# Two edits in a four-layer decoder on one core: the attention of layer 2 with split key sums, logarithm roots and shared copies, and a state-space loop whose softplus is put ahead of a masked copy

## The chip, the core and the metric

The kernel runs on one core of a Trainium2 chip. Five engines work side by side, each in the order of its own program: TensorE (PE, with its weight loads shown as PEld), VectorE (DVE), ScalarE (ACT), GpSimd (POOL) and SyncE (SP, which only starts transfers here). They wait for each other by semaphores. The metric is the device time of one launch in microseconds, the median of several runs. Lower is better.

## What is computed

The program is a decoder of four layers on x of shape 8 x 256 x 128, each with attention, cross attention and a feed-forward part. Two of its twelve stages are touched.

The state space (part of layer 1's attention) runs 4 Mamba layers over 8 sequences, 32 units in all. A unit has a step size by softplus, a causal convolution, a masked overlap of the B and C projections, decays, and a result that passes a gate and a norm.

The wide cross attention (layer 2) has 8 sequences of 256 queries and 256 keys, 16 heads of 64, with a mean-square norm of every head of queries and keys:

```python
def rms_norm(x, w):
    var = jnp.mean(jnp.square(x), axis=-1, keepdims=True)
    return x * jax.lax.rsqrt(var + EPS) * w
qh = rms_norm((q @ Wq).reshape(b, l, HEADS, HEAD_DIM).transpose(0, 2, 1, 3), q_norm_w)
kh = rms_norm((kv @ Wk).reshape(b, s, HEADS, HEAD_DIM).transpose(0, 2, 1, 3), k_norm_w)
vh = (kv @ Wv).reshape(b, s, HEADS, HEAD_DIM).transpose(0, 2, 1, 3)
scores = jnp.where(mask, jnp.einsum('bhld,bhsd->bhls', qh, kh) * (1.0 / np.sqrt(HEAD_DIM)), NEG_INF)
o = jnp.einsum('bhls,bhsd->bhld', jax.nn.softmax(scores, axis=-1), vh)
```

## The kernel before

Every stage hands each engine a list of instructions in a fixed order; nothing is scheduled at run time.

**The wide attention** (class `Wide`) has 64 steps: 8 sequences by 8 pairs of heads, w = 0 to 7. In step p, PE forms the scores of pair p in banks 0 and 1 (`score_pe`); DVE takes the row maxima and makes the exponential's biases (`maximum_dve`, L3045 and L3049); ACT takes the exponentials (`weigh_act`, L3150). PE's scores of step p+1 wait for these exponentials, since they use the same two banks. DVE then sums the exponentials of step p-1 (`inverse_dve`, L3065 to L3070), POOL scales them (`scale_pool`, L3241), PE turns those of step p-2 (`turn_pe`, L2928), DVE copies one bank of them and ACT the other (`copy_dve` L3056, `copy_act` L3159), and PE multiplies those of step p-3 by the values (`values_pe`).

Between these stand the pieces that prepare the next sequence, by a table: `SCHEDULE` says in which of the 8 steps each is done. P00 to P11 are the key projections (token half, column half), copied by ACT; Q0 to Q3 the queries; KS the sums of the squared keys over each head, whose squares POOL makes (`squares_pool`, L3236); KR a square root on ACT (L3174) and KD a reciprocal (L3085) and the scaling of the two key halves on DVE (L3089); T00 to T11 the turned keys, copied by DVE (L3111); M and X the queries' mean squares; QR and QD their root (L3177) and reciprocal (L3092); V0 to V3 the values, copied and masked by DVE (L3104); B0 and B1 the output product of the sequence before. The first two PE pieces of a step are "early": on each engine they stand after the exponentials (ACT) or the sums (DVE), and ahead of the copies of the turned weights. The others stand at the step's end. PE's pieces go through three banks in turn. The `Sqrt` of a root needs another table of ACT than the `Exp` of the steps, so a table load (ACT_TABLE_LOAD) stands ahead of each root and ahead of the next exponential.

**The state space** (class `StateSpace`) runs one iteration n per unit. In an iteration DVE does, in this order: the masked copy of the overlap (`overlap_dve`, L1902 and L1903, which waits for PE); the decays' product (`weights_dve`, L1908, the other half of which POOL does under the same line); the first tap of the convolution (L1890); the final product into XNT (`final_dve`, L1942); more taps (L1893); the sums (L1932, L1936); and the inputs (L1923). In every second iteration the softplus of the next two units is worked in between: five small operations (`start_dve`, L1594 to L1602) after the masked copy, four steps of a series (L1608) after the decays' product, and the rest after the first tap. The softplus starts from an exponential that ACT makes at the iteration's start (L1587).

Of the kernel before, what the change touches and what calls it, by code (L numbers as in the profile page):

```python
# [1631 lines left out]
class StateSpace:  # L1632
# [311 lines left out]
    def dve(self, dve):  # L1944
# [877 lines left out]
class Wide:  # L2822
# [12 lines left out]
    SCHEDULE = (("P00", "P01", "Q0"), ("P10", "P11", "Q1"), ("Q2", "Q3", "KS"), ("M", "V0", "KR", "KD"), ("B0", "V1"),  # L2835
                ("T00", "T01", "X"), ("T10", "T11", "V2", "QR", "QD"), ("B1", "V3"))
# [3 lines left out]
    def __init__(self, k):  # L2840
# [21 lines left out]
        on_pe = [piece for piece in self.place if piece[0] not in ("KS", "KR", "KD", "QR", "QD")]  # L2862
# [25 lines left out]
    def read(self, piece):  # L2888
# [3 lines left out]
        return signal.at(*piece)  # L2892
# [3 lines left out]
    def score_pe(self, pe, p):  # L2896
        s, (b, w) = self.k.s, divmod(p, NWIDE)
        q, key = self.side(self.Q, b), self.side(self.K, b)
        if w == 0:
            pe.wait_ge(*self.read(("Q3", b)))  # L2900
            pe.wait_ge(*self.read(("T11", b)))
# [32 lines left out]
    def values_pe(self, pe, p):  # L2934
        s, (b, w) = self.k.s, divmod(p, NWIDE)
        if w == 0:
            pe.wait_ge(*self.read(("V3", b)))
# [103 lines left out]
    def maximum_dve(self, dve, p, o):  # L3041
# [5 lines left out]
        if w == 0 and o == 0:  # L3047
            dve.wait_ge(*s.rstd.at("queries", b))
# [23 lines left out]
    def piece_dve(self, dve, piece):  # L3072
# [3 lines left out]
        if name == "KS":  # L3076
            for t in range(HALVES):
                dve.wait_ge(*s.pool.at("squares", b, t))
                dve.tensor_reduce(self.kms[:, t * H:(t + 1) * H], self.ksquares[t].rearrange("p (h d) -> p h d", d=HW), AXX,
                                  ALU.add).then_inc(*s.stats.up("keys", b, t))  # L3080
            dve.wait_ge(*s.stats.at("keys", b, HALVES - 1))
            dve.tensor_scalar(self.kms, self.kms, 1.0 / HW, 1e-5, ALU.mult, ALU.add).then_inc(*s.variance.up("keys", b))
        elif name == "KD":
            dve.wait_ge(*s.deviation.at("keys", b))
            dve.reciprocal(self.kms, self.kms).then_inc(*s.rstd.up("keys", b))  # L3085
            dve.wait_ge(*s.rstd.at("keys", b))
            for t in range(HALVES):
                x = self.raw[t].rearrange("p (h d) -> p h d", d=HW)
# [132 lines left out]
    def pool(self, pool):  # L3221
# [1108 lines left out]
```

## Time and profile before

| | |
|---|---|
| Time of the kernel before, median of 3 runs | 2303.56 us (2299.27 to 2307.39) |
| Profiled execution: its own time | 2310.8 us |
| Profiled execution: span from first to last instruction | 2309.0 us |
| Busy: PE, DVE, ACT, POOL | 1907.6, 1584.6, 1307.4, 646.3 us |
| Mean granted TensorE clock | 0.904 |
| State-space loop in the trace | about 521 to 960 us |
| Wide attention in the trace | about 1378 to 1797 us |

The span is the profiler's stretch from the first to the last instruction; 1.8 us of that execution lie around it. Busy time is a sum over stages with different limits, so each stage has to be read by itself.

### The profile page before, as it was taken

What the parts mean: (1) busy time and instruction counts of PE and PEld (TensorE: products, weight loads), DVE (VectorE), ACT (ScalarE), POOL (GpSimd) and SP (SyncE); (2) the same over time, 40 slices, a digit from 0 to 9 for tenths busy, and PEclk for the clock granted to TensorE, in tenths of its full rate; (3) what the DMA queues carried; (4) which work ended last, traced back from release to release, by engine and by line L of the source; (5) the groups of instructions that cost most, each with busy time, mean ns of one, the idle gap of its engine ahead of it and who ended that gap; (6) DMA issues with size and microseconds to landing.
All of it is one profiled execution on the core that took longest, in us unless ns stands there. A gap on an engine that the chain in (4) does not pass through costs nothing.

```text
span 2309.0 us, 37826 instructions
## 1 busy us (share of the span) xinstructions
PE 1907.6 (83%) x13360; PEld 1271.5 (55%) x13360; DVE 1584.6 (69%) x3689; ACT 1307.4 (57%) x2688; POOL 646.3 (28%) x616
## 2 busy tenths in 40 slices
PE   7999766979999999849864388899888997679886
PEld 5777652446777777524452254556555676434465
DVE  5777685866767767458659948888888457568543
ACT  5777433766777777517755236676665312337622
POOL 3332003104433333342004532334334001131043
PEclk9999887999999999969986689999999898779897
DMA  4000005400000000034101000000000100254112
GB/s 191 1 2 2 1 0 152 141 34 5 1 1 1 1 1 1 1 91 147 56 8 68 0 1 1 1 1 1 1 1 1 52 4 1 95 159 132 43 35 78
DMA packets 80155, 87.39 MB, mean 38 GB/s; under 512 B 6578, under 2 KB 70115, under 8 KB 79073
## 3 DMA queue, kind: packets, MB, share of 16 engines
q1 hardware_dynamic: 78625, 82.49, 11.3%
q0 software_dynamic: 1344, 2.49, 0.4%
q8 instruction: 109, 1.79, 0.3%
q14 instruction: 77, 0.63, 0.1%
HBM read 54.39 MB, written 30.70 MB: 37 GB/s over the span
## 4 chain that ended last, share of the span: by engine, by line
PE 50%; DVE 31%; issue 8%; POOL 5%; ACT 5%; DMA 2%; SPq 0%; DVEq 0%; POOLq 0%; ACTq 0%
PE bank L469 42%; DVE scratch L1221 5%; PE bank L653 2%; DVE scratch L3045 2%; DVE scratch L3065 2%; PE bank L368 2%; POOL w_early L3241 1%; DVE stats L245 1%; PE bank L693 1%; POOL w_early L3236 1%; DVE w_keep L1893 1%; DVE w_early L2497 1%; PE bank L1190 1%; DVE XN L3089 1%; DMA scratch<-parts 1%
## 5 line engine op out<-in xcount | busy, mean ns | idle before, releaser
L469 PE MATMUL bank<-scratch 64*128 64x256 bf16 (+7 forms) x3056 | 340.9, 307 | 83.2 <-DMA scratch<-parts 39.8
L1221 DVE TENSOR_REDUCE scratch<-bank 128x2 f32<-128x512 f32 x384 | 244.6, 686 | 83.5 <-PE bank L469 80.6
L469 PEld LDWEIGHTS bank<-scratch 64*128 64x128 bf16 (+4 forms) x3056 | 183.9, 122 | 212.1 <-DVE scratch L1221 73.6
L469 PE MATMUL bank<-w_keep,scratch 128*128 128x128 f32 (+4 forms) x1760 | 246.6, 331 | 26.8 <-DVE scratch L1936 12.1
L469 PE MATMUL bank<-XNT,w_keep 128*128 128x256 f32 (+4 forms) x800 | 238.6, 438 | 6.8 <-POOL w_keep L2131 4.6
L1307 ACT ACTIVATE w_keep<-bank 128x512 f32<-128x512 f32 x384 | 212.5, 597 | 53.6 <-PE bank L469 45.7
L469 PEld LDWEIGHTS bank<-w_keep,scratch 128*128 128x128 f32 (+3 forms) x1760 | 183.7, 185 | 92.9 <-issue 63.5
L469 PE MATMUL bank<-w_early,scratch 64*128 64x256 f32 (+3 forms) x1152 | 168.9, 355 | 42.4 <-ACT w_early L3150 26.0
L469 PEld LDWEIGHTS bank<-XNT,w_keep 128*128 128x128 f32 x800 | 150.2, 197 | 59.9 <-issue 30.4
L469 PEld LDWEIGHTS bank<-w_early,scratch 64*128 64x128 f32 (+3 forms) x1152 | 122.6, 189 | 89.2 <-issue 32.3
L469 PE MATMUL bank<-w_keep 128*32 128x256 f32 (+1 forms) x1600 | 125.2, 388 | 8.8 <-ACT w_keep L1307 5.4
L469 PE MATMUL bank<-scratch,w_early 128*128 128x256 f32 (+2 forms) x416 | 124.0, 442 | 10.2 <-DVE scratch L2492 3.8
L795 ACT ACTIVATE scratch<-bank,scratch 128x256 f32<-128x256 f32 x256 | 100.3, 475 | 54.9 <-DVE scratch L721 54.9
L3150 ACT ACTIVATE w_early<-bank,scratch 128x256 f32<-128x256 f32 x172 | 83.0, 563 | 84.3 <-DVE scratch L3049 84.2
L3241 POOL TENSOR_TENSOR w_early<-w_early,scratch 128x1024 f32<-128x1024 f32 x43 | 81.4, 1893 | 173.5 <-DVE scratch L3070 173.5
L721 DVE TENSOR_REDUCE scratch<-bank 128x2 f32<-128x512 f32 x128 | 82.5, 686 | 61.7 <-PE bank L469 61.6
L469 PE MATMUL bank<-XNT,w_early 128*128 128x256 f32 (+1 forms) x384 | 119.1, 441 | 4.5 <-ACT XNT L383 1.6
L368 PE MATMUL bank<-w_keep,XN 128*128 128x128 f32 x192 | 49.3, 435 | 78.9 <-DVE XN L318 76.1
L3045 DVE TENSOR_REDUCE scratch<-bank 128x2 f32<-128x512 f32 x128 | 87.6, 685 | 25.4 <-PE bank L469 25.2
L469 PEld LDWEIGHTS bank<-scratch,w_early 128*128 128x128 f32 x416 | 72.2, 199 | 51.2 <-issue 30.8
L469 PEld LDWEIGHTS bank<-XNT,w_early 128*128 128x128 f32 x384 | 73.2, 201 | 46.0 <-issue 32.1
L735 POOL TENSOR_TENSOR scratch<-scratch 128x1024 f32<-128x1024 f32 x32 | 61.5, 1951 | 127.2 <-DVE scratch L751 127.2
(452 smaller groups left out, 3974.5 us busy)
## 6 DMA issues: line engine op xcount, KB each, us to landing
scratch<-parts SPq DMA_DIRECT2D x24, 1024.0 KB, 5.0
parts<-scratch SPq DMA_DIRECT2D x192, 96.0 KB, 2.5
parts<-scratch SPq DMA_DIRECT2D x96, 64.0 KB, 2.1
w_early<-pack_l3f SPq DMA_DIRECT2D x1, 5206.0 KB, 16.3
w_keep<-pack_l2f SPq DMA_DIRECT2D x1, 2124.0 KB, 12.5
w_early<-pack_mamba SPq DMA_DIRECT2D x1, 2120.0 KB, 19.2
w_keep<-pack_l2x SPq DMA_DIRECT2D x1, 2049.0 KB, 7.8
w_keep<-taps SPq DMA_DIRECT2D x4, 512.0 KB, 5.6
```

Of the source, the lines that this page charges most:

```text
L368: t = pe.transpose(k.bank[q][:, j * P:(j + 1) * P], src(i), k.w["ident"])
L469: return pe.matmul(out, lhsT, rhs, start=start, stop=stop, skip_group_check=True)
L653: m = pe.transpose(self.k.bank[3 + o][:, c * S + t * P:c * S + (t + 1) * P], self.expo[g % 4][:, t * S + c * P:t * S + (c + 1) * P], self. ...
L721: dve.tensor_reduce(self.neg[g % 4], self.scores(g)[:, :].rearrange("p (t s) -> p t s", s=S), AXX, ALU.max, negate=True).then_inc(*s.maxed ...
L735: return pool.tensor_tensor(self.kron[n][t].rearrange("p (h i j) -> p h i j", i=HD, j=HD), a, c, ALU.mult)
L795: a = act.activation(self.expo[g % 4][:, t * S:(t + 1) * S], self.scores(g)[:, t * S:(t + 1) * S], ACT.Exp, bias=self.neg[g % 4][:, t:t + 1])
L1221: dve.tensor_reduce(neg[:, :, h], self.k.bank[5 - g % 2][:, :].rearrange("p (t s) -> p t s", s=S), AXX, ALU.max, negate=True).then_inc(*s. ...
L1307: act.activation(self.expo[g % 8], k.bank[g % 4][:, :], ACT.Exp, scale=HD ** -0.5).then_inc(*s.weighed.up("e", g))
L3045: dve.tensor_reduce(neg, self.k.bank[o][:, :].rearrange("p (t s) -> p t s", s=S), AXX, ALU.max, negate=True).then_inc(*s.maxed.up("x", p, o))
L3065: dve.tensor_reduce(sums, self.by_row(p), AXX, ALU.add).then_inc(*s.stats.up("sums", p))
L3150: a = act.activation(self.weights(p, o)[:, t * S:(t + 1) * S], self.k.bank[o][:, t * S:(t + 1) * S], ACT.Exp, bias=self.bias[p % 2][:, o * ...
L3241: pool.tensor_tensor(ex, ex, self.sums[p % 2].unsqueeze(2).to_broadcast([P, 2 * HALVES, S]), ALU.mult).then_inc(*s.pool.up("scaled", p))
```

## The change

Wide attention. KS becomes KS0 and KS1, one token half each, in steps 1 and 2, and POOL squares a half ahead of the scaling of its step instead of behind it. KR moves from step 3 to step 2, and takes `Ln` (with the mean's factor and the small constant inside) and `Exp` with factor -0.5 instead of `Sqrt`; so the reciprocal and the variance operation of DVE go, and no table load is left in the loop. KD becomes KD0 and KD1, in steps 3 and 4. QR does the same with `Ln` and `Exp`, and QD goes. V1, V3, T01 and T11 are copied by ACT instead of DVE. State space: the softplus' start and first four series steps stand ahead of the masked copy.

```diff
+            if soft:
+                soft.start_dve(dve, n)
+                soft.series_dve(dve, n, 0, 4)
             if there(prep):
                 self.overlap_dve(dve, prep)
-            if soft:
-                soft.start_dve(dve, n)
-            if there(prep):
                 self.weights_dve(dve, prep)
-            if soft:
-                soft.series_dve(dve, n, 0, 4)
...
-    SCHEDULE = (("P00", "P01", "Q0"), ("P10", "P11", "Q1"), ("Q2", "Q3", "KS"), ("M", "V0", "KR", "KD"), ("B0", "V1"),
-                ("T00", "T01", "X"), ("T10", "T11", "V2", "QR", "QD"), ("B1", "V3"))
+    SCHEDULE = (("P00", "P01", "Q0"), ("P10", "P11", "Q1", "KS0"), ("Q2", "Q3", "KS1", "KR"), ("M", "V0", "KD0"), ("B0", "V1", "KD1"),
+                ("T00", "T01", "X"), ("T10", "T11", "V2", "QR"), ("B1", "V3"))
+    ON_ACT = ("V1", "V3", "T01", "T11")
...
+        if name[0:2] == "KS":
+            t = digits[0]
+            dve.wait_ge(*s.pool.at("squares", b, t))
+            dve.tensor_reduce(self.kms[:, t * H:(t + 1) * H], self.ksquares[t].rearrange("p (h d) -> p h d", d=HW), AXX,
+                              ALU.add).then_inc(*s.stats.up("keys", b, t))
+        elif name[0:2] == "KD":
+            t = digits[0]
+            x = self.raw[t].rearrange("p (h d) -> p h d", d=HW)
             dve.wait_ge(*s.deviation.at("keys", b))
...
         if name == "KR":
-            act.wait_ge(*s.variance.at("keys", b))
-            act.activation(self.kms, self.kms, ACT.Sqrt).then_inc(*s.deviation.up("keys", b))
+            act.wait_ge(*s.stats.at("keys", b, 1))
+            act.activation(self.kms, self.kms, ACT.Ln, bias=k.small[:, 0:1], scale=1.0 / HW).then_inc(*s.scalar.up("keys", b))
+            act.wait_ge(*s.scalar.at("keys", b))
+            act.activation(self.kms, self.kms, ACT.Exp, scale=-0.5).then_inc(*s.deviation.up("keys", b))
...
+        elif name[0] == "V" and name in self.ON_ACT:
+            t, part = divmod(digits[0], 2)
+            act.wait_ge(*s.projected.at(*piece))
...
+            act.activation(self.values(b)[:, t, 8 * part:8 * part + 8, :], bank[:, :].rearrange("p (h d) -> p h d", d=HW), ACT.Copy,
+                           scale=self.keep[:, b * HALVES + t:b * HALVES + t + 1]).then_inc(*s.stacked.up(*piece))
...
         for p in range(self.STEPS):
             b, w = divmod(p, NWIDE)
-            self.scale_pool(pool, p)
             if w in (0, 1) and b + 1 < B:
                 self.squares_pool(pool, b + 1, w)
+            self.scale_pool(pool, p)
...
-        pre_norm_act(k, e, ACT.Exp)
+        pre_norm_act(k, e)
+        e.preload_act_table_set("natural_log_exp_and_others")
```

On DVE, in the state space's iteration with a softplus, the order changes as follows (L1902 and L1903 are the masked copy, L1594 to L1602 the softplus' start, L1608 its series, L1908 the decays' product):

```order
-L1902 TENSOR_TENSOR scratch<-bank,w_keep 128x256
-L1903 COPY scratch<-bank 128x128
 L1594 TENSOR_SCALAR scratch<-scratch 128x16
 L1596 RECIPROCAL scratch<-scratch 128x16
 L1598 TENSOR_TENSOR scratch<-scratch 128x16
 L1600 TENSOR_TENSOR scratch<-scratch 128x16
 L1602 TENSOR_SCALAR scratch<-scratch 128x16
-L1908 TENSOR_TENSOR scratch<-scratch 128x512
 L1608 SCALAR_TENSOR_TENSOR scratch<-scratch 128x16 x4
+L1902 TENSOR_TENSOR scratch<-bank,w_keep 128x256
+L1903 COPY scratch<-bank 128x128
+L1908 TENSOR_TENSOR scratch<-scratch 128x512
```

Nine small operations now stand ahead of the copy, and the copy and the product stand together.

On DVE in the wide attention, step 3 of a sequence before, from the sums of the exponentials (L3065) to the next step's maxima (L3045): L3104 is V0, L3056 the copy of the turned weights, L3085 and L3089 are KD.

```order
L3065 TENSOR_REDUCE scratch<-w_early 128x4
L3067 SCALAR_TENSOR_TENSOR scratch<-w_early,scratch 128x4
L3070 RECIPROCAL scratch<-scratch 128x4
L3104 TENSOR_SCALAR scratch<-bank,scratch 128x512
L3056 COPY scratch<-bank 128x512
L3085 RECIPROCAL scratch<-scratch 128x32
L3089 TENSOR_TENSOR XN<-XN,scratch 128x1024 x2
L3045 TENSOR_REDUCE scratch<-bank 128x2
```

The same stretch in the changed kernel, where L3100 is V0, L3057 the copy and L3086 KD0:

```order
L3066 TENSOR_REDUCE scratch<-w_early 128x4
L3068 SCALAR_TENSOR_TENSOR scratch<-w_early,scratch 128x4
L3071 RECIPROCAL scratch<-scratch 128x4
L3100 TENSOR_SCALAR scratch<-bank,scratch 128x512
L3057 COPY scratch<-bank 128x512
L3086 TENSOR_TENSOR XN<-XN,scratch 128x1024
L3046 TENSOR_REDUCE scratch<-bank 128x2
```

The reciprocal is gone, and the scaling of the second key half has moved into step 4, behind that step's copy; in both steps the sums, after which POOL starts its scaling, stand a copy and a value or output piece ahead of it.

On ACT in the wide attention, from the last copies of step 3 to the next exponentials before (L3174 is the keys' root, L3150 an exponential):

```order
L3159 ACTIVATE scratch<-bank 128x512
L3166 ACTIVATE CX<-bank 128x256
L3174 ACT_TABLE_LOAD
L3174 ACTIVATE scratch<-scratch 128x32
L3150 ACT_TABLE_LOAD
L3150 ACTIVATE w_early<-bank,scratch 128x256 x4
```

In the changed kernel the root stands at the end of step 2, as L3170 and L3172:

```order
L3155 ACTIVATE scratch<-bank 128x512
L3170 ACTIVATE scratch<-scratch,small 128x32
L3172 ACTIVATE scratch<-scratch 128x32
L3146 ACTIVATE w_early<-bank,scratch 128x256 x4
L3212 ACTIVATE w_early<-bank 128x512
```

Both table loads are gone from this place, and the root stands ahead of step 3's exponentials instead of behind them.

## Rows read from the trace of the kernel before

**Rows 1.** Busy time in the wide attention, with granted clock (windows, all engines)

```profile
core 0: us, PE busy (x) PEld busy (x) DVE busy (x) ACT busy (x) POOL busy (x), PEclk, DMA share, GB/s
...
1380.00:1785.00 405.00, 354.39 (x2264) 230.04 (x2264) 338.22 (x682) 268.39 (x529) 148.93 (x79) 0.96 0.00 1
```

**Rows 2.** Wide attention, PE in order of time: start, duration, idle before

```profile
1558.11 1.13 PE L469 MATMUL bank<-w_early,scratch 64*128 64x256 f32 x8
...
1562.99 1.70 PE L469 MATMUL bank<-w_early,scratch 64*128 64x256 f32 x16
...
1571.01 2.08 PE L469 MATMUL bank<-w_early,scratch 64*128 64x256 f32 x8 [2.94 <-ACT w_early L3150]
...
1579.63 1.14 PE L469 MATMUL bank<-w_early,scratch 64*128 64x256 f32 x8
...
1584.39 1.14 PE L469 MATMUL bank<-w_early,scratch 64*128 64x256 f32 x8
...
1589.82 1.14 PE L469 MATMUL bank<-w_early,scratch 64*128 64x256 f32 x8
...
1596.49 1.13 PE L469 MATMUL bank<-w_early,scratch 64*128 64x256 f32 x8 [0.81 <-ACT w_early L3150]
...
1602.42 1.13 PE L469 MATMUL bank<-w_early,scratch 64*128 64x256 f32 x8
```

**Rows 3.** Wide attention, DVE in order of time, steps 2 and 3

```profile
1559.28 0.69 DVE L3045 TENSOR_REDUCE scratch<-bank 128x2 f32<-128x512 f32 x1 [2.04 <-PE bank L469]
...
1566.76 1.22 DVE L3079 TENSOR_REDUCE scratch<-w_early 128x16 f32<-128x1024 f32 x1 [1.79 <-POOL w_early L3236]
...
1568.11 0.68 DVE L3045 TENSOR_REDUCE scratch<-bank 128x2 f32<-128x512 f32 x1
...
1571.32 0.74 DVE L3104 TENSOR_SCALAR scratch<-bank,scratch 128x512 f32<-128x512 f32 x1
...
1573.78 0.35 DVE L3085 RECIPROCAL scratch<-scratch 128x32 f32<-128x32 f32 x1 [1.12 <-ACT scratch L3174]
1574.17 2.36 DVE L3089 TENSOR_TENSOR XN<-XN,scratch 128x1024 f32<-128x1024 f32 x2
```

**Rows 4.** Wide attention, POOL in order of time: three of its 64 scalings

```profile
1407.19 1.89 POOL L3241 TENSOR_TENSOR w_early<-w_early,scratch 128x1024 f32<-128x1024 f32 x1 [19.49 <-DVE scratch L3070]
...
1571.48 1.89 POOL L3241 TENSOR_TENSOR scratch<-scratch 128x1024 f32<-128x1024 f32 x1 [4.76 <-DVE scratch L3070]
...
1756.24 1.89 POOL L3241 TENSOR_TENSOR scratch<-scratch 128x1024 f32<-128x1024 f32 x1 [2.51 <-DVE scratch L3070]
```

**Rows 5.** The bias operation, L3049: duration ns min/median/max

```profile
L3049 DVE TENSOR_TENSOR scratch<-scratch x128: 161/164/1216, 1400.5 to 1781.1; 128x2 f32<-128x2 f32 x128
```

**Rows 6.** State space, DVE in order of time: an iteration with softplus, one without

```profile
705.55 0.43 DVE L1902 TENSOR_TENSOR scratch<-bank,w_keep 128x256 f32<-128x256 f32 x1 [3.67 <-PE bank L469]
...
706.09 0.17 DVE L1594 TENSOR_SCALAR scratch<-scratch 128x16 f32<-128x16 f32 x1
...
706.57 0.98 DVE L1598 TENSOR_TENSOR scratch<-scratch 128x16 f32<-128x16 f32 x1
...
708.36 0.69 DVE L1908 TENSOR_TENSOR scratch<-scratch 128x512 f32<-128x512 f32 x1
708.96 0.80 DVE L1608 SCALAR_TENSOR_TENSOR scratch<-scratch 128x16 f32<-128x16 f32 x4
709.68 0.61 DVE L1890 TENSOR_SCALAR w_keep<-w_keep,w_early 128x256 f32<-128x256 f32 x2
...
711.42 0.42 DVE L1942 TENSOR_TENSOR XNT<-bank,scratch 128x256 f32<-128x256 f32 x1
...
720.83 2.09 DVE L1890 TENSOR_SCALAR w_keep<-w_keep,w_early 128x256 f32<-128x256 f32 x2
```

**Rows 7.** State space, POOL in order of time, the iteration with softplus

```profile
706.25 1.27 POOL L1908 TENSOR_TENSOR scratch<-scratch 128x512 f32<-128x512 f32 x1 [3.27 <-DVE scratch L1903]
```

**Rows 8.** State space, ACT in order of time: the softplus' exponential

```profile
703.54 0.21 ACT L1587 ACTIVATE scratch<-scratch 128x16 f32<-128x16 f32 x1
```

**Rows 9.** Who waited for whom, 540 to 940 us: total, times, longest

```profile
PE bank L469 <- DVE XNT L1942: 16.0, 14, 1.2
```

More of the change, by code:

```diff
@@ L2822 @@
 class Wide:
-    SCHEDULE = (("P00", "P01", "Q0"), ("P10", "P11", "Q1"), ("Q2", "Q3", "KS"), ("M", "V0", "KR", "KD"), ("B0", "V1"),
-                ("T00", "T01", "X"), ("T10", "T11", "V2", "QR", "QD"), ("B1", "V3"))
+    SCHEDULE = (("P00", "P01", "Q0"), ("P10", "P11", "Q1", "KS0"), ("Q2", "Q3", "KS1", "KR"), ("M", "V0", "KD0"), ("B0", "V1", "KD1"),
+                ("T00", "T01", "X"), ("T10", "T11", "V2", "QR"), ("B1", "V3"))
+    ON_ACT = ("V1", "V3", "T01", "T11")
+    UNBANKED = ("KS0", "KS1", "KR", "KD0", "KD1", "QR")
     LAG = 2
@@ L2861, in __init__ @@
                         self.place[name, b] = d * NWIDE + step if d >= 0 else -1
-        on_pe = [piece for piece in self.place if piece[0] not in ("KS", "KR", "KD", "QR", "QD")]
+        on_pe = [piece for piece in self.place if piece[0] not in self.UNBANKED]
         self.number = {piece: n for n, piece in enumerate(on_pe)}
@@ L2891, in read @@
         signal = {"P": s.stacked, "Q": s.stacked, "M": s.stacked, "V": s.formed, "T": s.formed, "X": s.formed, "B": s.added}[name[0]]
-        return signal.at(*piece)
+        return (s.stacked if name in self.ON_ACT else signal).at(*piece)
     def score_pe(self, pe, p):
@@ L2899, in score_pe @@
         if w == 0:
-            pe.wait_ge(*self.read(("Q3", b)))
+            pe.wait_ge(*self.read(("T10", b)))
             pe.wait_ge(*self.read(("T11", b)))
@@ L2936, in values_pe @@
         if w == 0:
+            pe.wait_ge(*self.read(("V2", b)))
             pe.wait_ge(*self.read(("V3", b)))
@@ L3047, in maximum_dve @@
         if w == 0 and o == 0:
-            dve.wait_ge(*s.rstd.at("queries", b))
+            dve.wait_ge(*s.deviation.at("queries", b))
         dve.tensor_tensor(bias, neg, self.root(b)[:, w // 4, :, w % 4, o], ALU.mult).then_inc(*s.biased.up("x", p, o))
@@ L3075, in piece_dve @@
         digits = [int(x) for x in name[1:] if x.isdigit()]
[L3076 to L3083, printed above, removed]
-            dve.wait_ge(*s.deviation.at("keys", b))
[L3085 to L3088, printed above, removed]
-                dve.tensor_tensor(x, x, self.kms[:, t * H:(t + 1) * H].unsqueeze(2).to_broadcast([P, H, HW]), ALU.mult).then_inc(*s.normed.up("keys", b, t))
-        elif name == "QD":
-            dve.wait_ge(*s.deviation.at("queries", b))
-            dve.reciprocal(self.qms[b % 2], self.qms[b % 2]).then_inc(*s.rstd.up("queries", b))
+        if name[0:2] == "KS":
[6 more added lines that the diff above has]
+            x = self.raw[t].rearrange("p (h d) -> p h d", d=HW)
+            dve.wait_ge(*s.deviation.at("keys", b))
+            dve.tensor_tensor(x, x, self.kms[:, t * H:(t + 1) * H].unsqueeze(2).to_broadcast([P, H, HW]), ALU.mult).then_inc(*s.normed.up("keys", b, t))
+        elif name in self.ON_ACT:
+            pass
         elif name[0] == "X":
@@ L3168, in piece_act @@
     def piece_act(self, act, piece):
-        s, (name, b) = self.k.s, piece
+        k, s, (name, b) = self.k, self.k.s, piece
         bank = self.bank(piece) if piece in self.number else None
@@ L3201, in act @@
         s = self.k.s
-        act.wait_ge(*s.vector.at("gain"))
+        act.wait_ge(*s.vector.at("keep"))
         for piece in self.pieces(-1):
```

13 lines of the change are left out of this document (12 added, 1 removed).

## The prediction

> **What bounds the kernel now.** The two stages have different limits, so I read each by itself, in this order: busy times by stretch, each engine in order of time, then who waits for whom.
>
> In the wide attention PE is busy 354 and DVE 338 of 405 us, at a mean granted clock of 0.96 [rows 1]. Neither is full, so the order of time has to tell. POOL's scaling of the first pair of heads stands at 1407.19 us for sequence 0 and at 1756.24 us for sequence 7 [rows 4]: seven sequences take 349.05 us, 49.9 each. In a middle one, PE's score groups mark the steps [rows 2]. PE itself works 5.93 us in step 0 (1596.49 to 1602.42), 4.88 in step 2, 5.08 in step 3 (1562.99 until it stops at 1571.01 less the 2.94 idle), 4.76 in step 5, 5.43 in step 6 and 5.86 in step 7 (without its 0.81 idle). Step 1 has the same pieces as step 0, and step 4 nearly those of step 7, 5.9. The sum is 43.8 us: what PE alone would take. The missing six us lie around step 3. DVE waits 1.79 us for POOL's squares in step 2 [rows 3], 1.12 us for ACT's root in step 3 [rows 3], and has much to do there; from one maximum at 1559.28 to the next at 1568.11 are 8.8 us. PE, whose scores need the exponentials behind those maxima, stands idle 2.94 us, and its next score group reads 2.08 us instead of 1.13 [rows 2]: the clock has fallen to its lower level for a moment. So this stage is DVE's, by steps 2 and 3, and PE would be next.
>
> In the state space PE waits for DVE's final product (L1942) in 14 iterations, 16.0 us in all [rows 9], about 1.15 each. That product stands at 711.42 us, late because the softplus is worked in ahead of it, while DVE sat idle 3.67 us just before, for PE's overlap [rows 6].
>
> **The change: state space.** The softplus' input is ready at 703.75 us (703.54 plus 0.21) [rows 8], DVE is idle until 705.55 [rows 6]. The nine operations now cost: the start from 706.09 to 708.36, 2.27 us, and four series steps from 708.96 to 709.68, 0.72 us [rows 6], 2.99 in all. But of the start, 0.8 us is L1598 alone, 0.98 us for 16 numbers a row where its neighbour L1594 takes 0.17 [rows 6]; it ends as POOL's 1.27 us product of 706.25 does [rows 7]. The next operation meets the POOL instruction behind. Ahead of the copy POOL has nothing of the kind to do, so I take 1.8 us: 703.8 to 705.6, which just fills the hole; the masked copy is late by 0.1 at most.
>
> From the copy to the final product are 5.87 us now (705.55 to 711.42). 2.99 leave. Something comes in: the first tap (L1890, two operations) takes 0.61 us here, but 2.09 in the iterations without softplus, where it meets POOL's product [rows 6]. With the softplus gone from in front of it, it meets it here too: plus 1.5. So 5.87 - 2.99 + 1.5 = 4.4, and with the 0.1 of lateness the product comes at 710.0 to 710.1 instead of 711.42: 1.3 earlier, which covers PE's wait of 1.15. Fourteen times that is the 16.0 us of [rows 9]. Bounds: nothing, if the softplus' start meets POOL again or ACT's exponential is late; 18 if PE's next waits shrink too. I take 16, the wait as measured.
>
> **The change: wide attention.** Costs by slot, from start to start. A bare DVE step is 3.8 us: maxima and sums 3.21 (1568.11 to 1571.32), and the copy, which with V0 ends at 1573.78 less 1.12, 1.34 for the two [rows 3]: 0.65 for a value piece, 0.6 for a copy. A key sum is 1.1 to 1.2 (L3079, 1.22), a key scaling 1.15 (half of L3089's 2.36) [rows 3]. Turned-key copies I take at 0.6 like the other copy, an output piece at 0.55.
>
> What leaves DVE per sequence: two value pieces 1.3, two key copies 1.2, reciprocals and variance 0.8, and the waits 1.79 and 1.12. What stays by step: 3.8, 4.9, 5.0, 5.6, 5.5, 4.5, 6.1, 4.3; sum 39.7 against PE's 43.8. ACT gains about four copies and two small operations, some 3 us, and loses the four table loads; where it waits for DVE's biases nearly every step it stays covered. Only step 2 brings it close (exponentials, Q2, Q3, copies and the root: 5.4 us). PE's program keeps its order and length.
>
> Would PE then run without a stop? The loop through the exponentials is short enough: maximum 1.17 after its score (1558.11 to 1559.28), next score 2.90 after the maximum (1568.11 to 1571.01) [rows 2, 3], 4.1 together, under PE's shortest step. By the steps alone, yes. But two small key operations move. KD0 and KD1 now stand 4.4 to 4.5 us behind the step's first maximum, and POOL's scaling begins 3.37 behind it (1568.11 to 1571.48) and takes 1.89 [rows 3, 4], so it is under way. Before, the scaling of 1571.48 was over when L3089 began at 1574.17. A DVE operation with two operands in SBUF that meets POOL seems to wait for it: L1598 above, and the bias operation, whose median is 164 ns and whose longest is 1216 [rows 5].
>
> The Trainium skill says so, and it speaks against this placing: "SBUF — State Buffer", section "Who interferes with whom", has a VectorE instruction with two SBUF inputs shut out while a GpSimd instruction reads SBUF, for all of that instruction. The traced L1598 agrees (0.98 us). By that rule a sequence takes the 45.6 us worked out next; if KD escaped it, 43.8.
>
> So KD0 ends at 5.22 + 1.15 = 6.4 behind its step's maximum instead of 5.6, and KD1 likewise, 6.4 instead of 5.5. The squares, which POOL now makes directly behind a scaling in steps 0 and 1, hold the next step's first bias operation by 0.3 and 0.6 us. Followed step by step (score at t, maximum at D, D the later of t + 1.17 and the end of DVE's step, next t the later of PE's end and D + 2.90), with t = 0 in step 0: scores at 5.9, 11.9, 16.8, 21.9, 28.2, 34.4, 39.8, and 45.6 for the next sequence; maxima at 1.2, 7.1, 13.0, 18.6, 25.0, 31.4, 36.0, 42.1. PE stops only ahead of step 6, for 1.4 us. The same rule with the steps of before gives 50.1, where 50.2 is seen, so I add 0.2 a sequence for what it lacks. Sequence 0 has no output pieces: 44.6. Six times 45.6, plus 44.6, plus 1.4: 319.6 against 349.05, a gain of 29.5. Sequence 7 has no pieces at all but outputs; it stays as it is. The first sequence's preparation loses a table load and a reciprocal on its chain and shares copies, all of which I put at 2 us (0 to 3, the load being 1.3 and the rest already beside PE).
>
> Sum: 16 + 29.5 + 2 = 47.5 us. Against the profiled execution, 2310.8 us with 1.8 around its span, that gives 2263.3; the median of the runs is 7.2 lower than that execution, so 2303.56 - 47.5 = 2256.
>
> **Rivals.** (a) As forecast, 2249 to 2263: 0.55. (b) KD is not held by POOL, or the holds fall into slack: PE runs through, 43.8 a sequence and 42.8 for sequence 0, a gain of 43.5, so 2242; against it L1598 and the longest L3049. 0.13. (c) PE's pause ahead of step 6 grows past what the clock forgives. A pause of 2.94 us brought the lower level, and score groups of 2.08 us; 0.81 did not [rows 2]. The low level cost the score group 0.95 us, and I count as much for the piece behind it: 1.9 us in each of six sequences, or as much in new small waits on the key sums or roots, makes 2268; my 1.4 lies between. 0.15. (d) The softplus ahead of the copy pays nothing, because the copy, and with it POOL's product and the tap, come later by as much: 2272. 0.10. (e) Both gains melt to under 7 us together: 0.04. (f) The other side, by one mechanism, the clock. If the new rhythm gave PE four pauses of over 2 us a sequence instead of one, each with the 1.9 of (c) behind it, seven sequences would lose 4 x 3.9 x 7 = 109 us, and with the gains of 47.5 the time is 2365. It decides from 54.5 lost, 7.8 us a sequence. The steps above have one pause, not four: 0.03. That the change does not do what it says is excluded for the loads: its order on ACT has none in the loop.
>
> 0.3% of the time, 7 us, is about what a measurement here can tell from nothing. Faster is (a) to (d), 0.93; within it (e), 0.04; slower (f), 0.03. The range must leave out at most 2 in 10: from (b)'s 2242, a us below for the 18 of the state space, to (d)'s 2272, plus one: 2241 to 2273.
>
> **What would show it.** L1598 near 0.17 us in nearly all iterations, L1890 near 2.1 in all, PE's wait for L1942 gone. In the wide attention no table load, no wait for the squares, key scalings of 1.9 to 2.1 us instead of 1.2, scaling of pair 0 every 45.6 us, PE idle mostly ahead of step 6, granted clock near 1.0. I am wrong if PE's step work is longer than read (its ends are modelled), if ACT becomes late in step 2 or 3, or if the copies that ACT takes over hold a bank that PE wants.

## The result, and the profile after

The changed kernel takes 2250.05 us (median of 4 runs, 2242.86 to 2250.55) against 2303.76 us for the one before beside it (2299.27 to 2307.39): a ratio of 0.9761, 95% interval 0.9734 to 0.9787. That is 53.7 us less; 47.5 were forecast. The profiled execution took 2249.74 us (span 2247.9, mean granted clock 0.913).

The busy times by stretch of the changed kernel: the stretch that holds the state space, the wide attention up to POOL's first scaling, its seven sequences, and its end.

```profile
core 0: us, PE busy (x) PEld busy (x) DVE busy (x) ACT busy (x) POOL busy (x), PEclk, DMA share, GB/s
337.03:981.93 644.90, 572.41 (x4000) 400.03 (x4000) 456.15 (x1174) 449.88 (x958) 219.16 (x215) 0.94 0.11 30
1347.47:1382.60 35.13, 28.99 (x120) 16.84 (x122) 20.70 (x46) 22.17 (x45) 5.68 (x3) 0.84 0.00 0
1382.60:1697.40 314.80, 295.18 (x1992) 190.68 (x1990) 288.17 (x553) 215.64 (x478) 130.05 (x69) 1.00 0.00 1
1697.40:1738.49 41.09, 32.91 (x248) 23.30 (x244) 29.51 (x62) 20.44 (x44) 15.14 (x8) 0.96 0.01 1
```

Cut at the same operations (a layer norm's variance, the first scalings of sequences 0 and 7), the two profiled executions compare so, in us:

| stretch | before | after | less |
|---|---|---|---|
| the one with the state space | 667.39 | 644.90 | 22.5 |
| in it, a pair of iterations, one with softplus and one without | 26.97 | 25.70 | 1.27 |
| wide attention to its first scaling | 36.0 | 35.2 | 0.8 |
| seven sequences | 349.05 | 314.8 | 34.3 |
| in them, a middle sequence | 50.2 | 45.35 | 4.9 |
| end of the wide attention | 41.1 | 41.1 | 0 |
| everything else | 1215.5 | 1212.0 | 3.5 |

In the wide attention PE now is busy 295 of 315 us at a granted clock of 1.00, where [rows 1] had 354 of 405 at 0.96. PE in order of time, in a middle sequence, shows all of its pauses:

```profile
1563.95 1.14 PE L469 MATMUL bank<-w_early,scratch 64*128 64x256 f32 x8
...
1568.83 1.70 PE L469 MATMUL bank<-w_early,scratch 64*128 64x256 f32 x16
...
1573.86 1.14 PE L469 MATMUL bank<-w_early,scratch 64*128 64x256 f32 x8
...
1579.87 1.14 PE L469 MATMUL bank<-w_early,scratch 64*128 64x256 f32 x8
...
1582.29 1.09 PE L2928 MATMUL bank<-w_keep,scratch 128*128 128x128 f32 x8 [0.26 <-POOL scratch L3255]
...
1586.13 1.13 PE L469 MATMUL bank<-w_early,scratch 64*128 64x256 f32 x8 [1.15 <-ACT w_early L3146]
...
1588.56 1.09 PE L2928 MATMUL bank<-w_keep,w_early 128*128 128x128 f32 x8 [0.27 <-POOL w_early L3255]
```

The 2.94 us that PE stood idle in step 3 and the score group of 2.08 us behind them [rows 2] are gone. So is what followed that group, sixteen matmuls that were also at the lower level; before and after they read:

```profile
1573.02 3.78 PE L469 MATMUL bank<-w_keep,CX 128*128 128x128 f32 x16
...
1574.92 2.05 PE L469 MATMUL bank<-w_keep,scratch 128*128 128x128 f32 x16
```

From score group to score group, step 3 falls from 8.02 to 5.03 us, which is the pause, and step 4 from 8.62 to 6.01, which is nearly all clock. More than half of the 4.9 us that a sequence gains is thus the clock behind the pause and not the pause; steps 5 to 7 together give 0.7 back. Step 2 keeps its 4.88. One pause of some size is left, 1.15 us ahead of step 6, where the forecast had 1.4. With 0.26 and 0.27 for two scalings that is 1.68, and 45.35 less 1.68 is 43.7 us of PE's own work, forecast as 43.8.

On DVE, in order of time, one finds what holds those exponentials back (L3071 is the reciprocal that POOL's scaling waits for, L3050 the bias operation, L3086 a key scaling):

```profile
1556.39 0.18 DVE L3071 RECIPROCAL scratch<-scratch 128x4 f32<-128x4 f32 x1
...
1559.92 0.49 DVE L3050 TENSOR_TENSOR scratch<-scratch 128x2 f32<-128x2 f32 x1
...
1565.84 0.82 DVE L3050 TENSOR_TENSOR scratch<-scratch 128x2 f32<-128x2 f32 x1
...
1575.17 1.88 DVE L3086 TENSOR_TENSOR XN<-XN,scratch 128x1024 f32<-128x1024 f32 x1
...
1581.27 2.04 DVE L3086 TENSOR_TENSOR XN<-XN,scratch 128x1024 f32<-128x1024 f32 x1
```

and on POOL, beside the last two:

```profile
1574.08 1.89 POOL L3255 TENSOR_TENSOR w_early<-w_early,scratch 128x1024 f32<-128x1024 f32 x1 [3.03 <-DVE scratch L3071]
...
1580.34 1.89 POOL L3255 TENSOR_TENSOR scratch<-scratch 128x1024 f32<-128x1024 f32 x1 [4.37 <-DVE scratch L3071]
```

Key scalings last 1.88 and 2.04 us, where half of L3089's 2.36 was 1.18 [rows 3]. POOL's scaling runs from 1574.08 to 1575.97, and the key scaling issued at 1575.17 ends at 1577.05, 1.08 behind it: it reads like one that could not begin until POOL was through. All fourteen key scalings of the seven sequences end 1.08 or 1.09 us behind the end of a POOL scaling, whether they were issued 0.43 or 1.09 us behind its start. The bias operation shows the squares that POOL now makes earlier, as 0.49 and 0.82 instead of 0.16, so held by 0.33 and 0.66 (forecast 0.3 and 0.6).

In the state space, DVE in order of time, an iteration with softplus:

```profile
697.24 0.18 DVE L1594 TENSOR_SCALAR scratch<-scratch 128x16 f32<-128x16 f32 x1 [1.90 <-ACT scratch L1587]
...
697.74 0.17 DVE L1598 TENSOR_TENSOR scratch<-scratch 128x16 f32<-128x16 f32 x1
...
699.10 0.42 DVE L1902 TENSOR_TENSOR scratch<-bank,w_keep 128x256 f32<-128x256 f32 x1
...
700.37 2.10 DVE L1890 TENSOR_SCALAR w_keep<-w_keep,w_early 128x256 f32<-128x256 f32 x2
...
703.61 0.42 DVE L1942 TENSOR_TENSOR XNT<-bank,scratch 128x256 f32<-128x256 f32 x1
```

L1598 takes 0.17 us instead of 0.98, and the two taps 2.10 instead of 0.61, as [rows 6] had them in the other iterations. From the copy to the final product are 4.51 us (forecast 4.4, before 5.87). Who waits for whom, 540 to 930 us, in total, times and longest:

```profile
PE bank L469 <- DVE scratch L1936: 10.5, 15, 1.7
PE bank L469 <- DVE XNT L1942: 1.3, 1, 1.3
```

Of PE's 14 waits for the final product [rows 9] one is left, the first, ahead of the steady rhythm; 13 are gone. The wait for L1936 is the one that stays, 0.63 us in a pair where it was 0.71; in total it was 12.1 us before.

### The profile page after: what moved, and what is told of

It is laid out like the page before. It is cut to its first block, busy times and chain, and to the rows that moved or that the text cites. A ratio compares the mean times of both kernels' runs of the same rounds, so it can differ in the third digit from the quotient of the medians.

```text
span 2247.9 us, 37788 instructions
## 1 busy us (share of the span) xinstructions
PE 1885.0 (84%) x13360; PEld 1256.4 (56%) x13360; DVE 1581.0 (70%) x3633; ACT 1284.4 (57%) x2705; POOL 654.6 (29%) x616
## 4 chain that ended last, share of the span: by engine, by line
PE 53%; DVE 29%; ACT 6%; issue 6%; POOL 2%; DMA 2%; SPq 0%; DVEq 0%; POOLq 0%; ACTq 0%
PE bank L469 45%; DVE scratch L1221 5%; PE bank L653 2%; ACT XN L1994 2%; PE bank L2928 2%; PE bank L368 2%; DVE scratch L3046 1%; DVE w_keep L1890 1%; DVE scratch L3066 1%; DVE stats L245 1%; PE bank L693 1%; DVE XN L3086 1%; DVE w_keep L1893 1%; DVE w_early L2495 1%; PE bank L1190 1%
## 5 line engine op out<-in xcount | busy, mean ns | idle before, releaser
L469 PE MATMUL bank<-w_keep,scratch 128*128 128x128 f32 (+4 forms) x1760 | 245.4, 330 | 24.9 <-DVE scratch L1936 10.5
L469 PE MATMUL bank<-XNT,w_keep 128*128 128x256 f32 (+4 forms) x800 | 238.1, 437 | 6.9 <-POOL w_keep L2129 4.7
L1893 DVE SCALAR_TENSOR_TENSOR w_keep<-w_keep,w_early 128x256 f32<-128x256 f32 x192 | 96.6, 552 | 0.1
```

What stands on the lines that cost most here:

```text
L469: return pe.matmul(out, lhsT, rhs, start=start, stop=stop, skip_group_check=True)
L1893: o = dve.scalar_tensor_tensor(out=yv[:, j, :], in0=xv[:, j, tap:tap + S], scalar=scale, in1=yv[:, j, :], op0=ALU.mult, op1=ALU.add)
```

## The experiments

All ratios are to the kernel before, run beside each. "Pair" is the pair of iterations of the table above, "sequence" a middle one of the seven, "wide attention" the whole stage in the trace, its preparation and end included.

| kernel | median us (range) | ratio [95%] | pair | sequence | wide attention |
|---|---|---|---|---|---|
| softplus_only | 2287.33 (2279.7–2290.04) | 0.9921 [0.9897, 0.9945] | 25.70 | 50.23 | 426.1 |
| wide_only | 2263.75 (2261.26–2271.09) | 0.9842 [0.9806, 0.9879] | 26.97 | 45.35 | 391.0 |
| keys_first | 2247.54 (2235.24–2249.26) | 0.976 [0.9729, 0.9791] | 25.70 | 44.08 | 383.7 |
| tap_first | 2251.13 (2247.98–2254.09) | 0.9775 [0.9741, 0.9808] | 25.74 | 45.35 | 391.0 |
| copies_on_dve | 2257.99 (2251.7–2262.61) | 0.9806 [0.977, 0.9842] | 25.70 | 46.84 | 400.6 |
| squares_behind | 2287.78 (2281.91–2294.12) | 0.9928 [0.9904, 0.9952] | 25.70 | 50.4 | 426.3 |
| square_roots | 2265.19 (2264.5–2268.43) | 0.9835 [0.98, 0.9871] | 25.70 | 47.7 | 404.8 |
| keys_again | 2248.55 (2241.27–2250.21) | 0.9749 [0.9723, 0.9774] | 25.70 | 44.08 | 385.2 |
| after_again | 2243.05 (2239.85–2252.6) | 0.974 [0.9712, 0.9768] | 25.70 | 45.35 | 389.8 |
| both_first | 2248.35 (2236.62–2251.87) | 0.9749 [0.9721, 0.9776] | 25.74 | 44.08 | 385.3 |

The kernel before took 2305.23 us beside rows one to four, 2304.9 beside rows five to seven and 2305.29 beside rows eight to ten; its wide attention took 426.1 us.

**One part of the change at a time.** softplus_only is the kernel before with the state space's edit alone; wide_only is the changed kernel with that edit undone, so:

```diff
+            if there(prep):
+                self.overlap_dve(dve, prep)
             if soft:
                 soft.start_dve(dve, n)
-                soft.series_dve(dve, n, 0, 4)
             if there(prep):
-                self.overlap_dve(dve, prep)
                 self.weights_dve(dve, prep)
+            if soft:
+                soft.series_dve(dve, n, 0, 4)
```

> The kernel before with the state space's edit alone. My theory: the two edits sit in different stages and add up, and this one takes PE's wait for the final product, 1.15 us in each of 14 iterations, and a little of the next wait: a pair of units in 25.7 us instead of 26.97, some 19 to 22 us in all, so about 2283; L1598 at 0.17 us and L1890 at 2.1 us in every iteration; the wide attention as before. Rival: the gain in the state space comes in part from the other edit or from run-to-run differences; then it is 8 us or less.

> The changed kernel with the softplus put back behind the masked copy. My theory: the wide attention's gain stands alone, 31 to 35 us, a sequence in 45.3 us instead of 50, so about 2270; the state space as before, 26.97 us a pair. Rival: the two edits share a resource or a clock state, and this run differs from the changed kernel by clearly more or less than what the other run gains (sum of the two gains off by over 7 us from 54).

Measured: 17.9 us for the first (2305.23 to 2287.33) and 41.5 for the second. Each part's rhythm is the same alone as with the other: 25.70 us a pair with either wide attention, 45.35 a sequence with either state space. The sum, 59.4, and the 53.7 of both together differ by no more than the intervals (5.5 to 8.4 us to either side) allow. The second is larger than the 31 to 35 us that I had expected, but in the trace the stage itself is 35.1 us shorter (391.0 for 426.1); the rest lies in code that was not touched.

The medians are too coarse for the size of the state space's part, so I take it from the trace. From the first unit's final product to the last one's are 384.91 us in wide_only and 368.33 in the changed kernel, 16.6 less: thirteen pairs at 1.27, and no change in the last iterations. In softplus_only, keys_first, keys_again and after_again it is 368.3 to 369.1. Ahead of the first product nothing is clearly won (237.4 us of the stretch in wide_only, 235.8 to 238.1 in these five). The stretch as a whole is a poorer witness; in wide_only, where nothing in it was changed, it took 660.76 us instead of 667.39. The kernel before had two pieces of that stretch at the lower clock:

```profile
core 0: us, PE busy (x) PEld busy (x) DVE busy (x) ACT busy (x) POOL busy (x), PEclk, DMA share, GB/s
...
959.17:969.41 10.24, 9.16 (x13) 3.94 (x14) 1.12 (x2) 3.66 (x6) 0.53 (x1) 0.50 0.00 0
552.98:556.39 3.41, 3.41 (x12) 1.97 (x9) 1.34 (x2) 3.02 (x5) 3.33 (x4) 0.50 0.02 5
```

**Key scalings away from POOL.** KD0 and KD1 stand directly behind the step's two maxima, ahead of the sums of the exponentials that POOL's scaling waits for.

```diff
                 self.maximum_dve(dve, p, 1)
+            early, late = self.split(p)
+            keys, late = [x for x in late if x[0][0:2] == "KD"], [x for x in late if x[0][0:2] != "KD"]
+            for piece in keys:
+                self.piece_dve(dve, piece)
             if 0 <= p - 1 < self.STEPS:
                 self.inverse_dve(dve, p - 1)
-            early, late = self.split(p)
```

> The changed kernel with KD0 and KD1 on DVE directly behind their step's maxima, ahead of the sums, so that they are done before POOL's scaling starts. Theory of the shared port (KD held by POOL's scaling): L3086 falls from 1.88 and 2.04 us to 1.22 in the loop, PE's pauses ahead of steps 5 and 6 shrink, a sequence takes 43.8 to 44.3 us instead of 45.3, total 7 to 10 us less than the changed kernel, about 2241 to 2243. Rival: the durations of 1.9 and 2.0 come from the operation itself in its new place (its operands, half the tile each) or from ACT or PE reading the same tile: then they stay and so does the time.

The key scaling in keys_first (min, median, max in ns):

```profile
L3086 DVE TENSOR_TENSOR XN<-XN,scratch x16: 1216/1219/1221, 1361.6 to 1655.6; 128x1024 f32<-128x1024 f32 x16
```

and in the changed kernel:

```profile
L3086 DVE TENSOR_TENSOR XN<-XN,scratch x16: 1215/1893/2544, 1367.4 to 1672.3; 128x1024 f32<-128x1024 f32 x16
```

The same sixteen operations of the same size take 1.22 us each where POOL does nothing, and up to 2.54 where its scaling runs. The sequence falls to 44.08 us, within 0.3 of rival (b)'s 43.8: that rival priced rightly what the hold costs, 1.3 us a sequence, and is wrong of the changed kernel only in that the hold is there. The median, 2247.54 us, does not show it (2241 to 2243 was expected); more on that below.

**The first tap ahead of the masked copy.** The same reasoning in the state space: L1890 takes 2.10 us where it meets POOL's product, so it is issued before that product's inputs are made.

```diff
                 soft.series_dve(dve, n, 0, 4)
+            if there(conv):
+                self.tap_dve(dve, conv, 0)
             if there(prep):
                 self.overlap_dve(dve, prep)
                 self.weights_dve(dve, prep)
-            if there(conv):
-                self.tap_dve(dve, conv, 0)
```

> The changed kernel with the first tap (L1890) ahead of the masked copy in every iteration, where DVE waits for PE and POOL reads nothing. Theory: L1890's 2.1 us are a wait for POOL's product; it falls to 0.6 us for two, DVE gets to L1936 over 1 us earlier and PE's wait of 0.64 us for it goes in 15 pairs: 9 us less than the changed kernel, about 2241. Rival: the tap's input from ACT is late there, or the masked copy and POOL's product behind it are delayed by the tap and the wait only moves: no change, or up to 0.6 us a pair slower.

The taps are free, and the pair is no shorter, 25.74 us. DVE in order of time, an iteration without softplus and one with:

```profile
687.29 0.62 DVE L1890 TENSOR_SCALAR w_keep<-w_keep,w_early 128x256 f32<-128x256 f32 x2 [2.66 <-ACT w_keep L2018]
...
690.30 0.17 DVE L1863 TENSOR_TENSOR scratch<-bank,w_early 128x16 f32<-128x16 f32 x1 [1.14 <-PE bank L469]
691.33 0.42 DVE L1942 TENSOR_TENSOR XNT<-bank,scratch 128x256 f32<-128x256 f32 x1 [0.85 <-PE bank L469]
...
700.84 0.61 DVE L1890 TENSOR_SCALAR w_keep<-w_keep,w_early 128x256 f32<-128x256 f32 x2
...
702.62 2.14 DVE L1608 SCALAR_TENSOR_TENSOR scratch<-scratch 128x16 f32<-128x16 f32 x3
```

The two iterations fail for different reasons. In the first the hold is gone, but PE does not wait for DVE in this iteration, and what DVE won it spends waiting for PE, 1.14 and 0.85 us. In the second PE does wait for DVE, for L1936, but there the hold has only moved to what stands next beside POOL's product, three series steps of 16 numbers a row: 2.14 us, where the changed kernel has 0.58 for them. From the softplus' first operation to L1936 DVE takes 9.10 us, in the changed kernel 9.07. So PE's wait is the same (11.1 us in the stretch, 10.5 in the changed kernel). A version with the hold taken off this iteration altogether was not run.

**The copies back on DVE.**

```diff
-    ON_ACT = ("V1", "V3", "T01", "T11")
+    ON_ACT = ()
```

> The changed kernel with V1, V3, T01 and T11 copied by DVE again (2.5 us of DVE a sequence). My step rule: the value copy stands ahead of KD1 and mostly fills its wait for POOL, so steps 5, 6 and 7 alone grow; a sequence in 46.0 to 46.3 us instead of 45.3, total 4 to 6 us more than the changed kernel, about 2255. Rival: DVE's 2.5 us count in full, as in a stage bound by DVE: 2.5 x 7 = 17 us more, about 2267.

A sequence is 1.5 us longer, half as much again as the most that I expected, and the total 8 us (4 to 6 expected). PE's pauses in one sequence, in order of time:

```profile
1550.13 1.13 PE L469 MATMUL bank<-w_early,scratch 64*128 64x256 f32 x8 [0.64 <-ACT w_early L3146]
1567.51 1.70 PE L469 MATMUL bank<-w_early,scratch 64*128 64x256 f32 x16 [0.58 <-ACT w_early L3146]
1581.12 1.09 PE L2928 MATMUL bank<-w_keep,scratch 128*128 128x128 f32 x8 [0.26 <-POOL scratch L3255]
1584.96 1.14 PE L469 MATMUL bank<-w_early,scratch 64*128 64x256 f32 x8 [1.15 <-ACT w_early L3146]
```

Two are new, 0.64 and 0.58; with the others they are 2.63 us against 1.68, which accounts for 0.95 of the 1.5. From score group to score group, step 7 is 0.71 longer than in the changed kernel, step 2 0.65 and step 3 0.16, and the others are as they were: all of the 1.5, and not in steps 5, 6 and 7 as I had expected. The 0.58 has a cause that the same place on DVE shows:

```profile
1555.21 0.18 DVE L3071 RECIPROCAL scratch<-scratch 128x4 f32<-128x4 f32 x1
...
1557.95 1.28 DVE L3050 TENSOR_TENSOR scratch<-scratch 128x2 f32<-128x2 f32 x1
...
1564.00 1.49 DVE L3050 TENSOR_TENSOR scratch<-scratch 128x2 f32<-128x2 f32 x1
```

PE's group of 1567.51 waits for the exponentials that stand behind the bias operation of 1564.00, held until 1565.49. From the reciprocal to the end of a held bias operation are 4.02 us (1555.21 to 1559.23), and in the changed kernel too (1556.39 to 1560.41), though the operation itself reads 1.28 here and 0.49 there. What is fixed is the chain from DVE's reciprocal (1555.21) over POOL's scaling (1555.47 to 1557.36) and its squares (1557.32 to 1559.22) to the end of the bias operation (1559.23). A later DVE cannot catch up in it.

**The squares behind the scaling again.**

```diff
         for p in range(self.STEPS):
             b, w = divmod(p, NWIDE)
+            self.scale_pool(pool, p)
             if w in (0, 1) and b + 1 < B:
                 self.squares_pool(pool, b + 1, w)
-            self.scale_pool(pool, p)
```

> The changed kernel with POOL's squares behind the scaling of their step again, all else kept. My step rule: each key sum waits some 3.3 us at the end of its step for a square that POOL starts only after a scaling; a sequence in about 50.5 us, all of the wide attention's gain gone, total 35 to 38 us more, about 2287. Rival: the order on POOL matters little since the key sums are split and a step's slack takes the wait: within 8 us of the changed kernel.

With everything else of the change in place, the sequence goes back to 50.4 us, where the kernel before has 50.2. DVE, in order of time:

```profile
1545.94 1.22 DVE L3080 TENSOR_REDUCE scratch<-w_early 128x16 f32<-128x1024 f32 x1 [3.27 <-POOL w_early L3250]
```

and PE behind it:

```profile
1549.98 1.32 PE L469 MATMUL bank<-w_early,scratch 64*128 64x256 f32 x8 [3.16 <-ACT w_early L3146]
```

The key sum waits 3.27 us for the squares, and the maxima, which stand behind it, hold the exponentials and PE. So with the sums at their new places in the table, splitting them, sharing the copies and dropping the loads give nothing unless POOL makes the squares ahead of the step's scaling. This order is a condition for the rest and not a part with a gain of its own: the first sum was moved up to step 1, where it needs its squares earlier.

**Square roots and their loads back**, with ACT's Sqrt and DVE's reciprocals at the places of the logarithm roots:

```diff
-            act.activation(self.kms, self.kms, ACT.Ln, bias=k.small[:, 0:1], scale=1.0 / HW).then_inc(*s.scalar.up("keys", b))
-            act.wait_ge(*s.scalar.at("keys", b))
-            act.activation(self.kms, self.kms, ACT.Exp, scale=-0.5).then_inc(*s.deviation.up("keys", b))
+            act.activation(self.kms, self.kms, ACT.Sqrt, bias=k.small[:, 0:1], scale=1.0 / HW).then_inc(*s.deviation.up("keys", b))
```

> The changed kernel with Sqrt on ACT and the reciprocals on DVE in place of Ln and Exp, the pieces in the changed kernel's steps (KR in step 2, the reciprocals ahead of KD0 and at the end of step 6). Table loads come back, 2 x 1.28 us in steps 2 and 6. My step rule: ACT comes late to the exponentials of step 3 by some 2 us, which the pause ahead of step 6 takes in part; a sequence in 46.3 us, total 5 to 7 us more, about 2256. Rival: the loads are the heart of the gain and cost in full, 5.1 us a sequence: 35 us more, about 2285.

It costs 2.35 us a sequence, more than twice what I expected. ACT, in order of time, has two loads of 1.28 us ahead of the exponentials that PE's next score group needs:

```profile
1532.85 1.28 ACT L3176 ACT_TABLE_LOAD   x1
...
1534.49 1.28 ACT L3152 ACT_TABLE_LOAD   x1
```

PE waits for them, and its clock falls (windows of the stretch behind the pause, and of the rest of the sequence):

```profile
1537.77 2.08 PE L469 MATMUL bank<-w_early,scratch 64*128 64x256 f32 x8 [2.65 <-ACT w_early L3152]
```

```profile
1537.77:1542.27 4.50, 4.50 (x24) 3.67 (x25) 2.93 (x6) 2.66 (x7) 0.00 (x0) 0.63 0.00 0
1542.27:1581.70 39.43, 39.11 (x262) 25.25 (x260) 35.51 (x72) 30.09 (x60) 16.95 (x9) 1.00 0.00 1
```

The pause of 2.65 us stands ahead of step 4. The 1.15 ahead of step 6 is gone, one of 0.29 stands ahead of the next sequence's step 0. Behind the pause of 2.65 us PE works 4.50 us at a granted clock of 0.63 on average; the score group alone is 0.94 longer. What I had priced was the pause, not the clock after it: the pauses listed are 2.94 us in all instead of 1.68, so 1.26 more, near the 1.0 that I had, and the 4.50 us of work take 2.95 in the changed kernel, 1.55 more. (Gaps too short for the list are some 0.5 us less.)

This is the price of the loads in the changed kernel's places, not what they cost before. There the keys' two loads stood ahead of an exponential that waited for DVE even so:

```profile
1577.36 1.93 ACT L3150 ACTIVATE w_early<-bank,scratch 128x256 f32<-128x256 f32 x4 [2.31 <-DVE scratch L3049]
```

That root could move up to step 2 without this cost because it needs no load. The kernel before with the logarithm roots alone was not run.

**Is there a faster version?** keys_again is keys_first, after_again the changed kernel, both_first has the key scalings and the tap moved together.

> The same kernel as keys_first, beside the changed kernel on one chip. If the 7.3 us that its wide stage was shorter are worth their full size, its median lies 5.5 to 7.5 us below that of the changed kernel in the same call (about 2243 against 2250); if the gain is given back outside the stage (the tail of the stage 1.9 us longer, or a lower clock elsewhere) it lies within 3 us of it.

> The changed kernel once more, beside keys_again: 2247 to 2252 us, with a wide attention stage of 391 us and 45.35 us per sequence. What keys_again differs by is read against this run, not against a run of another call.

> Keys' scaling ahead of the root's bias operation and the first tap ahead of the masked copy together. As the tap's move alone was worth nothing (25.74 against 25.70 us per pair of units), it should equal keys_again within 3 us, with 44.08 us per wide sequence and 25.7 us per pair; a further gain of 2 us or more would say that the tap's move pays where the key's does.

Not by the time measured: 2248.55 and 2248.35 us against 2243.05, where I had expected the former 5.5 to 7.5 below or at worst within 3. Over all its runs the version with the key scalings moved has ten with a median of 2248.1, the changed kernel nine with 2244.9, and the ranges lie over each other (2235.2 to 2250.2, 2239.9 to 2252.6). The seven sequences are 8.7 us shorter, though. Windows of keys_again over the seven sequences and the end, and below them those of after_again:

```profile
1386.00:1692.00 306.00, 292.72 (x1982) 191.08 (x1980) 278.83 (x553) 215.88 (x476) 130.13 (x70) 1.00 0.00 1
1692.00:1736.02 44.02, 36.12 (x256) 24.79 (x252) 28.91 (x62) 20.92 (x45) 15.08 (x8) 0.91 0.01 1
```

```profile
1375.90:1690.60 314.70, 296.58 (x1990) 192.04 (x1988) 288.05 (x553) 215.85 (x477) 130.07 (x70) 0.99 0.00 1
1690.60:1730.49 39.89, 31.13 (x246) 22.13 (x242) 29.24 (x62) 20.22 (x43) 14.91 (x8) 1.00 0.00 1
```

Half of the gain is given back at once: the end of the stage, which has no key pieces, takes 44.02 instead of 39.89 us, at a granted clock of 0.91 instead of 1.00. In it keys_again has a pause of 1.28 us, and the group behind is at the lower level, 1.84 us instead of 1.09 (a second such place is behind a pause of 1.77 us at 1723.52, 1.86 for 1.09):

```profile
1699.62 1.84 PE L2928 MATMUL bank<-w_keep,w_early 128*128 128x128 f32 x8 [1.28 <-POOL w_early L3258]
```

after_again has the same pause without that:

```profile
1687.90 1.09 PE L2928 MATMUL bank<-w_keep,w_early 128*128 128x128 f32 x8 [1.28 <-POOL w_early L3255]
```

This is not one unlucky run. From sequence 7's first scaling the end takes 42.92, 44.09 and 44.10 us in keys_first, keys_again and both_first, the three with the key scalings moved, and 40.14 or 41.1 in the kernel before and all the other versions of the table. So 2 to 4 of the 8.7 us are given back each time, at a granted clock of 0.95, 0.91 and 0.91 instead of 0.96 or 1.00, though nothing in the end's own code differs. What in the earlier sequences brings this about is not shown.

The rest of the difference lies outside the stage, in code that is the same. The state space's stretch took 647.55 us in keys_again and 642.59 in after_again, but 643.13 in keys_first, of the same code as the former. So that difference comes from the run; that a small edit shifts how often it comes is neither shown nor excluded by ten runs. No version has a median clearly below that of the change as it was made. The whole wide attention was 4.5 to 7.3 us shorter in the three, its end included, and the total does not show it.

## Why the prediction was right

**State space, forecast 16, measured 16.6.** The mechanism went step by step as written: L1598 at 0.17, the taps at 2.10, the copy to the product 4.51 (4.4), the wait for L1942 gone in all pairs but the first. I had counted 14 waits of 1.15 us; 13 went, and a pair lost 1.27, since the wait for L1936 behind it shrank by 0.08 too ("if PE's next waits shrink too" was the upper bound, 18). The two small errors cancel. Rival (d), that the softplus ahead of the copy pays nothing, is refuted by softplus_only. Its median is 17.9 us lower, with 5.5 to either side, which agrees (I had expected 19 to 22).

**Wide attention, forecast 29.5, measured 34.3.** The single pause, its place and nearly its size (1.15 us for 1.4), PE's own 43.7 us, the key scalings' 1.9 to 2.0 us, the two holds of the bias and the clock at 1.00 are as forecast. The sum came 4.8 us too high, in three places of "Six times 45.6, plus 44.6, plus 1.4: 319.6". The walk by steps gave 45.6 for a middle sequence and 45.35 was measured: 1.5 us over six. The "I add 0.2 a sequence for what it lacks", 1.4 over seven, was not needed. And the last of the seven was 48.58 us in the kernel before already, some 1.7 shorter than its neighbours, and is 43.50 now; I had given it the full length, 1.9 too much, of which the sequence before it, 0.3 longer than the others, gives some back. Sequence 0, 44.24 for 44.6, makes up the rest. So the mechanism was right, and the term was mis-sized by a correction that the walk did not want and by one sequence at its end. One time in the walk does not follow from its own rule: the score of step 5 is put at 28.2, where the maximum at 25.0 plus 2.90 and PE's 21.9 plus 5.9 give 27.9 at most. The pause ahead of step 6 would then be some 1.6 and not 1.4 us; the 45.6 stay, since step 6 starts from DVE.

**The preparation, forecast 2, measured 0.8.** On the low side of its 0 to 3.

**POOL's hold of DVE**, which separated the forecast from rival (b), is shown by keys_first: the same operation 1.22 us away from POOL, and with a median of 1.89 beside it. By the Trainium skill's "SBUF — State Buffer", section "Who interferes with whom", a VectorE instruction with two SBUF inputs is shut out for all of a GpSimd instruction that reads SBUF; the 1.88 us above, ending 1.08 behind POOL's end, agrees. tap_first shows what else it takes to gain by this: the engine behind must be waiting for DVE, and no other operation of the kind may take the place beside POOL.

**The clock**, rivals (c) and (f). Pauses of 1.15 us in every sequence left it at 1.00. square_roots shows that the mechanism of (c) is there: a pause of 2.65 us was followed by 0.63 on average over the next 4.50 us. A pause of 1.28 was followed by the lower level in keys_again and not in after_again, so no bound between can be read from these runs. The price that (c) put on the clock was too low. It counts 0.95 us for the score group and as much for the piece behind it, but that piece was 1.73 longer in the kernel before (3.78 for 2.05); step 4 lost 2.6 us in all, not 1.9.

**What of the 53.7 I could not have forecast.** The parts that were changed give 16.6 + 34.3 + 0.8 = 51.7 us, close to the difference of the medians. The two profiled executions lie further apart, 61.1 us by their spans: 3.5 of the rest are outside both stages, and 5.9 in the stretch with the state space, beside its pairs. That stretch differs as much between kernels with the same code in it (667.39 and 660.76 us), with pieces at a lower granted clock in the longer one.

## What to carry to other kernels

Walk a pipelined stage step by step, with the end of each engine's step as the start of the next: it gave 45.6 us against a measured 45.35, and put the remaining pause at its place; mean busy shares would have given neither. When pricing a pause of TensorE, look at all that runs behind it: here the slower clock cost nearly as much as the pause (2.6 us behind 2.94). Before moving a VectorE operation, look what GpSimd does beside the new place, which operation takes the old one, and whether anyone waits for VectorE there: the same cure paid 1.3 us a sequence in one stage and nothing in the other. When parts of an edit feed each other, undo each in the finished version: here the order of two POOL instructions, a small thing in the diff, decides on the whole gain of the stage.

## What the runs showed of the hardware

- A hold by POOL falls on small operations too: three series steps on 16 numbers a row read 2.14 us in tap_first at 702.62, beside POOL's product, and 0.58 in the changed kernel at 702.39, behind it.
- L1890, a TENSOR_SCALAR on 128x256, is held as well: 0.61 to 0.62 us for two away from POOL, 2.10 beside it.
- A key scaling of 1.22 us, issued while POOL's scaling ran, ended 1.08 or 1.09 us behind the scaling's end in 14 of 14 cases.
- The end of the wide attention ran at a lower granted clock in all three versions with the key scalings moved, 0.91 to 0.95 instead of 0.96 to 1.00, and took 1.8 to 4.0 us longer, though its code was the same.
